# A graph network layer: 48 products for receivers in one group behind twelve rounds, or in six shares of eight behind the last six of them

## What is computed

```python
in_agg = jax.ops.segment_sum(edge_feat, receivers, num_segments=N_NODES)
out_agg = jax.ops.segment_sum(edge_feat, senders, num_segments=N_NODES)
to_updater = jnp.concatenate([in_agg, out_agg, node_feat], axis=1)
h = jax.nn.relu(to_updater @ W1 + b1)
return h @ W2 + b2          # then x = layernorm(x + that)
```

## Time and profile before

| what | before |
|---|---|
| median of 3 runs | 1528.48 us (1525.78 to 1528.65) |
| the profiled execution, own time | 1530.54 us |
| its span, first to last instruction | 1528.7 us |
| PE busy | 1379.1 us, 90% |
| DVE busy | 1357.8 us, 89% |
| GpSimd busy | 1209.9 us, 79% |
| ScalarE busy | 1015.3 us, 66% |
| mean granted clock of TensorE | 0.992 |

### The profile page before, as it was taken

The page is one execution under the profiler, slowest core; times in us unless marked ns, Lnnn a source line. Parts: engine busy times, 40 slices in busy tenths (PEclk is TensorE's granted clock), DMA queues, the critical chain, the costliest instruction groups (busy, mean ns, idle before and its releaser), DMA issues.

```text
span 1528.7 us, 63755 instructions
## 1 busy us (share of the span) xinstructions
PE 1379.1 (90%) x23554; PEld 1066.2 (70%) x23555; DVE 1357.8 (89%) x3561; ACT 1015.3 (66%) x2193; POOL 1209.9 (79%) x667
## 2 busy tenths in 40 slices
PE   3329999999999999999999899999999999999896
PEld 2128888888888888888888766565656566565442
DVE  6989999999999999999999899998999999998564
ACT  5417777777777777777777667666766667676442
POOL 2888888888888888888888688888888888888433
PEclk9999999999999999999999899999999999999998
DMA  8227777777777777777778777677766677666531
GB/s 295 27 14 170 174 176 177 176 176 177 177 176 176 176 176 176 175 175 188 202 201 203 194 196 186 159 186 168 195 181 168 168 195 195 161 149 168 109 104 39
DMA packets 216732, 255.50 MB, mean 167 GB/s; under 512 B 99469, under 2 KB 179356, under 8 KB 216392
## 3 DMA queue, kind: packets, MB, share of 16 engines
q1 hardware_dynamic: 123482, 223.88, 44.7%
q0 software_dynamic: 92960, 28.90, 22.0%
q10 hardware_dynamic: 144, 0.67, 0.2%
HBM read 143.18 MB, written 110.21 MB: 166 GB/s over the span
## 4 chain that ended last, share of the span: by engine, by line
PE 87%; DVE 6%; issue 4%; ACT 1%; DMA 1%; POOL 0%; DVEq 0%; ACTq 0%
PE psum L1464 37%; PE psum L1486 30%; PE psum L1441 7%; PE psum L1537 3%; PE psum L1448 2%; PE psum L1535 2%; PE psum L1608 1%; PE psum L1602 1%; PE psum L1619 1%; PE psum L1510 1%; PE psum L1511 1%; DMA cst<-in_consts 1%; DVE to_node L1176 1%; DVE from_group L1011 1%; DVE in_group L1046 0%
## 5 line engine op out<-in xcount | busy, mean ns | idle before, releaser
L665 POOL DMA_INDIRECT out_tables<-payload,target x632 | 1176.4, 1861 | 242.8 <-issue 185.1
L1464 PE MATMUL psum<-parts,to_slot 128*128 128x194 bf16 x6552 | 587.0, 247 | 0.7 <-ACT slots_out L760 0.7
L1464 PEld LDWEIGHTS psum<-parts,to_slot 128*128 128x128 bf16 x6552 | 553.3, 97 | 17.0 <-issue 1.0
L1486 PE MATMUL psum<-to_node,slots_in 64*64 64x448 bf16 x9828 | 481.6, 351 | 5.3 <-ACT halves_sum L842 3.5
L1486 PEld LDWEIGHTS psum<-to_node,slots_in 64*64 64x64 bf16 x9828 | 289.9, 107 | 175.4 <-ACT halves_sum L842 5.8
L760 ACT ACTIVATE slots_out<-psum 128x388 bf16<-128x388 f32 (+1 forms) x936 | 367.3, 474 | 54.6 <-PE psum L1464 46.6
L1137 DVE TENSOR_SCALAR to_slot<-iota_h,slot 128x896 bf16<-128x896 f16 x940 | 378.6, 455 | 0.0
L1176 DVE TENSOR_SCALAR to_node<-iota_h,slot_rel 128x448 bf16<-128x448 f16 x819 | 268.8, 346 | 6.3 <-PE psum L1486 6.2
L779 ACT ACTIVATE payload<-psum 128x256 f32<-128x256 f32 x158 | 60.9, 386 | 270.4 <-PE psum L1537 263.4
L1176 DVE TENSOR_SCALAR to_node<-iota_rows,slot_rel 128x448 bf16<-128x448 f16 x546 | 236.7, 433 | 0.0
L811 ACT ACTIVATE to_node<-apart 128x448 bf16<-128x448 bf16 x273 | 149.3, 575 | 71.0 <-PE psum L1486 68.5
(11 more groups left out here) (128 smaller groups left out, 800.4 us busy)
## 6 DMA issues: line engine op xcount, KB each, us to landing
slot_tiles<-slots_out SPq DMA_DIRECT2D x78, 1018.5 KB
feat<-in_edge_attr SPq DMA_DIRECT2D x195, 256.0 KB
slots_in<-slot_tiles SPq DMA_DIRECT2D x40, 970.0 KB
slots_in<-slot_tiles SPq DMA_DIRECT2D x40, 921.5 KB
out_tables<-payload,target POOLq DMA_INDIRECT x632
out_tables<-zeros POOLq DMA_DIRECT2D x4, 1600.0 KB
feat<-out_tables SPq DMA_DIRECT2D x48, 128.0 KB
slots_in<-slot_tiles SPq DMA_DIRECT2D x14, 242.5 KB
```

Source lines behind the costliest of these rows:

```text
L665: e.indirect_dma_start(out_tab, at, payload[b][:, t, :], None, element_offset=k * TABLE_ROWS * D, compute_op=ALU.add).then_inc(s_tab[k], 16)
L1464: last = e.matmul(ps_share[r % BANKS][:, o:o + SLOT_W], to_slot[m][:, k, g * P:(g + 1) * P], parts[b][:, SHARE_FROM + MINI * m + k, 1:], s ...
L1486: return e.matmul(ps_share[bank_no + h][cols, 0:HOT], slots_in[p % RING][rows, j - PART_FROM[p], D * k:D * (k + 1)], to_node[rows, node_bu ...
```

## The change

`sum_windows` gets a number n and issues only the n-th of six shares, eight products each; what it waits for stands ahead of the first share, and the signal behind the last. In the sharing chunks a share stands behind each of the rounds 6 to 11. In the early and summing chunks the six shares follow each other, which is the order of before.

```diff
+WINDOW_SHARES = 6
...
-            def sum_windows(c, b):
-                e.wait_ge(s_hot, HALVES * (c + 1))
-                e.wait_ge(s_wadd, HALVES * c + 2)
-                e.nop(nofuse=True)
-                for j in range(HALF):
-                    for k in range(3):
-                        for h in range(HALVES):
-                            t = HALF * h + j
-                            last = e.matmul(ps_win[b][h], parts[b][:, t, 1 + k * D:1 + (k + 1) * D], onehot[b][:, t // 2, :, t % 2],
-                                            start=(j == 0 and k == 0), stop=(j == HALF - 1 and k == 2))
-                last.then_inc(s_quad, QUADS)
+            def sum_windows(c, b, n):
+                if n == 0:
+                    e.wait_ge(s_hot, HALVES * (c + 1))
+                    e.wait_ge(s_wadd, HALVES * c + 2)
+                    e.nop(nofuse=True)
+                steps = HALF * 3 // WINDOW_SHARES
+                for step in range(steps * n, steps * (n + 1)):
+                    j, k = divmod(step, 3)
+                    for h in range(HALVES):
+                        t = HALF * h + j
+                        last = e.matmul(ps_win[b][h], parts[b][:, t, 1 + k * D:1 + (k + 1) * D], onehot[b][:, t // 2, :, t % 2],
+                                        start=(step == 0), stop=(step == HALF * 3 - 1))
+                if n == WINDOW_SHARES - 1:
+                    last.then_inc(s_quad, QUADS)
...
                         for r in range(MINIS * q, MINIS * q + MINIS):
                             slot_round(at, b, r)
+                            if r >= CHUNK_ROUNDS - WINDOW_SHARES:
+                                sum_windows(c, b, r - (CHUNK_ROUNDS - WINDOW_SHARES))
                     if mode.window:
-                        if q == QUADS - 1:
+                        if q == QUADS - 1 and not mode.share:
...
-                            sum_windows(c, b)
+                            for n in range(WINDOW_SHARES):
+                                sum_windows(c, b, n)
```

## The result

The changed kernel takes 1593.88 us (median of 4 runs, 1592.81 to 1595.32), the kernel before, run beside it, 1528.57 us (4 runs): a ratio of 1.043 (1.042 to 1.045). It is slower by 65 us. I had forecast 1546 us, and the range 1534 to 1567 does not hold it.

The account below looks back on a forecast made before the run. TensorE was taken to bound the kernel. Per chunk, window products rise from 1.79 to 2.02 us; over 78 chunks 17 us, added to 1530.5 gives 1547.6, less 2.1 for the median: 1546 us, range 1534 to 1567.

Parts of the forecast that it names:

- The crossings: Ten added tile-shape changes per chunk between slot and window products on TensorE, claimed to cost 1.03 us a chunk.
- the Trainium skill's rule alone: Each tiling mode change drains TensorE with nothing given back: ten added drains a chunk, 80 us slower.
- What is given back: Mid-group stall and loop jump around the window products on TensorE, both claimed to vanish, returning 0.80 us a chunk.
- a hiccup of TensorE's own sequencer: Claimed cause of the 0.32 us idle behind the 40th or 41st window product, hidden once long products are queued.
- The cover for the jump: At a pass's end, the last 17 queued products give 0.87 us, enough to hide the loop jump's 0.66 us.
- rival 1: The cover fails: the loop jump, perhaps the mid-group stall too, still shows; 1562 up to 1587 us, chance 0.17.
- ScalarE's evacuation gets more time per round, not less: ScalarE's copies of slot sums were claimed to gain time in each round; no cost was put on this.
- a new wait of TensorE for VectorE's to_slot: Sign of being wrong: VectorE's to_slot tiles delay TensorE; at least 0.4 us of slack was claimed.
- VectorE's wait for the split: Sign of being right: VectorE's 0.6 us wait per chunk for ScalarE's split grows by 0.2 us.
- Crossings that are nearly free: Rival: tile-shape changes inside slot rounds cost almost nothing, so the change saves 69 us, to 1459; faster had chance 0.10.
- No change: Rival: a shorter crossing out or a covered TensorE wait makes both kernels meet within 3 us; chance 0.05.
- The side: The whole kernel's direction: slower, given chance 0.85, against faster 0.10 and same 0.05.

Follow-up runs that it names:

- e2: Kernel before, with SyncE's store of a sharing chunk's slot sums issued one round later: 1589.78 us, ratio 1.040.
- e18: Kernel before without GpSimd's four scatters (indirect DMAs) of each sharing chunk: 1475.73 us against 1530.87 for the kernel before in its job, ratio 0.964.
- e9: Kernel before, unchanged, run again in another job: 1481.33 us, ratio 0.998.
- e17: Changed kernel without GpSimd's four scatters of each sharing chunk: 1554.68 us against 1532.79 for the kernel before in its job, ratio 1.014.
- e10: Changed kernel, unchanged, run again in a job where the kernel before took 1481.33 us: 1549.26 us, ratio 1.043.
- e3: Changed kernel with ScalarE's copy of round 0 ahead of the split and the node table: 1555.37 us, ratio 1.019.
- e4: Changed kernel with all 48 window products in one piece behind round 8 instead of six shares: 1494.68 us, ratio 0.977 to the kernel before.
- e15: Same kernel as e4, run again in another job: 1473.16 us, ratio 0.995 to the kernel before.
- e8: Changed kernel with the window products in one piece behind round 8 and ScalarE's copy of round 0 ahead of its first split: 1498.17 us, ratio 1.011.
- e7: Changed kernel with three shares of sixteen window products behind rounds 9, 10 and 11 instead of six of eight: 1511.19 us, ratio 1.020.
- e14: Changed kernel without GpSimd's four scatters of each sharing chunk, in the same job as e13: 1548.51 us, ratio 1.046.
- e13: Kernel before without GpSimd's four scatters of each sharing chunk, in the same job as e14: 1472.01 us, ratio 0.994.

## Why the prediction was wrong

A chunk by the starts of TensorE's products, mean over 67 to 72 chunks of each trace (those that begin between 150 and 850 us), in us: the chunk; from the last slot product ahead of window products to the next product behind them, summed; the longest step inside a share or group; and the step to the 29th slot product, the first of round 4, which is 0.086 where nothing is waited for.

```
kernel                             job     chunk  windows  longest step  29th step
before                             late     9.62    1.90       0.52        0.10
before, store later (e2)           late    10.37    1.86       0.47        0.90
before without scatters (e18)      late     8.92    1.20       0.05        0.10
before (e9)                        prompt   8.97    1.22       0.05        0.14
after                              late    10.43    2.56       0.05        0.63
after without scatters (e17)       late     9.91    2.56       0.05        0.11
after (e10)                        prompt   9.90    2.56       0.05        0.10
after, round 0 first (e3)          late     9.94    2.56       0.05        0.09
group behind round 8 (e4)          late     9.14    1.29       0.21        0.24
group behind round 8 (e15)         prompt   8.91    1.07       0.05        0.23
the same, round 0 first (e8)       prompt   9.20    1.07       0.05        0.09
three shares (e7)                  prompt   9.40    1.83       0.05        0.10
```

**The crossings: right, and a little small.** A step in is 177 ns over 426 places, a step out 128 ns over 284, eight products 0.12 us, all within 4 ns of what I took. The ten added crossings cost a chunk 9.907 less 8.916, plus the 0.13 us of jump that e18 still shows and e17 does not: 1.12 us, where I had 1.03. That is 0.11 us each. (e17 and e18 are of two jobs; e14 and e13, of one, give the same 0.99 between chunks.) More than half of the excess over my sum, 0.05 us, lies in the slot products' own steps, some 10 ns on the first of them behind a crossing. Three shares have four more crossings than one group and pay 0.11 us each as well (9.40 less 8.79, less 0.17 of jump, over 4). The Trainium skill ("TensorEngine Tiling (Array Packing)", Key Properties) says that a change of the tiling mode drains TensorE. The trace agrees: it is paid at every crossing. The rows of the weight loads (PEld) of the changed kernel show the overlap that is lost:

```profile
512.87 0.21 PEld L1444 LDWEIGHTS psum<-onehot,parts 128*64 128x64 bf16 x8 [0.16 <-issue]
513.12 0.20 PEld L1468 LDWEIGHTS psum<-parts,to_slot 128*128 128x128 bf16 x3
```

The load of a share's first weights starts at 512.87, with the product itself (2 ns ahead by the records), and so does that of the next slot product at 513.12 (4 ns ahead); between two slot products the load starts some 84 ns ahead of its product. By the Trainium skill's rule alone, at the rows' price, I had worked out 80 us; e17 stands 79 us over e18.

**What is given back: right in the amount, the gap's part with a wrong cause.** Gap and jump give back 9.62 less 8.79, 0.83 us, against the 0.80 that I had. For the gap I was lucky: I let it go because a queue of long products would cover a hiccup of TensorE's own sequencer, and it was no such hiccup (below). The cover for the jump, 0.87 us of work against 0.66, held (rival 1 did not come), and e7 shows its edge: with sixteen short products at the end of a chunk instead of eight, 0.17 us of it comes through in the mean. So the net of the two is 1.12 less 0.83, 0.29 us a chunk, 22 us in all, where I had 0.22 and 17. The e17 kernel measures just this: 21.9 us over the kernel before in its job.

**The step that failed: "ScalarE's evacuation gets more time per round, not less. ... Nothing here is priced."** For rounds 6 to 11 this is so, but the bank of round 4 is freed by the copy of round 0, and no share stands between these. From the last of the 12 products TensorE needs 2.41 us to the 29th slot product. ScalarE needs 0.23 us to its payload and 2.07 from there to the end of round 0's copy (505.21 to 506.79 + 0.49), 2.30 in all, and with the signal and the product's own start behind it that is 2.43: in the kernel before the 29th step is 0.105 us in every one of 72 chunks, where it is 0.086 once round 0 comes first (e3). The wait was already there, by 0.02 us; the list of waits has none of these, only one of 0.7 us. With the signal 0.53 us late there is no slack to take it, and TensorE pays all: 0.53 us by 78 chunks, 41 us. With the 22 us that is 63; measured 65. Among my signs of being wrong stood a new wait of TensorE for VectorE's to_slot; the new wait is for ScalarE. VectorE's wait for the split, which I expected to grow by 0.2 us, stayed at 0.6 (44.1 us in 75 against 45.2 in 77).

**The cause behind it, which I had put in the wrong place.** I took the gap in the group for a hiccup of TensorE's own sequencer, which short products bare and long ones cover. It is the mark of a scatter's start, and so is the late signal. In the kernel before the scatters fell, by the phase of the chunk, on the window group and on signals of rounds that nobody was waiting for closely. In the changed kernel no share shows a gap, and the same interference fell on the one signal with no slack behind it. e2 shows that this needs no share: a shift of the store does it.

**Rivals.** Crossings that are nearly free: refuted by every row. No change: refuted. The side was right at 0.85, for a sum of which one term was missing. In the prompt jobs no gap is given back, and the change costs 0.93 us a chunk, the crossings less the part of the jump that they hide: 1549 us, next to my 1546 by no merit of mine, since it starts from 1481.

**What is left open.** By which way a scatter holds a TensorE signal, and why only in some jobs; the scatters' own records are alike in both. From when on a signal is held: in e2 those due from 0.28 us after the fourth scatter's start come late, in the kernel before those due 0.56 to 0.65 us after it are on time. Why scatters of 1.6 to 1.9 us hold signals and those of 2.2 to 2.5 us mostly don't; e4's gap of 0.21 us follows one of 2.18 us, at 1.40 to 1.61 us after its start, in 71 of 72 chunks, and is absent from the prompt e15. The kernel before has no trace in the two last jobs, so that they are late is read from its time. And the changed kernel with and without scatters was not run in one late job.

**The better version.** One group behind round 8 gains 2.3% in a late job (e4) and 0.5% in a prompt one (e15). It adds no crossing, has 20 long products ahead of the jump (windows 1.07 us against 1.22), and in the late job the gap in it is 0.21 us instead of 0.52.

## What to carry to other kernels

- Where products of two tile shapes share TensorE, count the crossings before the products: 0.1 us each here, as much as seven of the short products that were moved. Move such work in one piece, to a place with long products on either side.
- For each moved stretch ask of every bank that is reused: which copy frees it, what stands ahead of that copy on its engine, and by how much it is early now. A wait that reads 0.7 us in all can be one without any slack; a single step that is 0.02 us longer than its neighbours gave it away.
- A gap that stands at one product number in a loop may still be another engine's. Compare its distance to the starts of the other engines' transfers before giving it a cause, in more than one kernel (in a periodic loop many starts keep a constant distance), and leave that transfer out once, in a job in which the gap is seen.

## What the runs showed of the hardware

- In the traces of the late jobs TensorE's completion signals that fell due some 0.8 to 1.3 us after the start of a GpSimd indirect DMA of 1.6 to 1.9 us (in e2's trace from 0.28 us on) came at about 1.30 to 1.40 us after it, 0.5 us late in the changed kernel and up to 1.0 us in e2. Long products went on starting meanwhile; window products of 16 ns each stood still from 0.75 to 1.27 us. Without these DMAs it was gone: 55 us of 1531 in the kernel before. No trace of the three prompt jobs shows it.
- A completion signal without interference comes 0.207 us after the start of the last of the 12 products (0.206 to 0.209 over 72 chunks of e18).
- At a change between 128x128 and 128x64 tiles the weight load of the next product started 2 to 4 ns ahead of it, against some 84 ns between slot products, and each added change cost a chunk 0.11 us (e17 against e18, e7).
- Window products, two to a pair in two halves of the columns, start 16 ns apart in the mean (0.767 us for the 47 steps of an undisturbed group, e18): 3 ns inside a pair and 30 from pair to pair.
